# One score ahead of a turned tile on TensorE, and one more copy of a turned tile on VectorE in every fifth unit of an attention kernel

## The reference, cut to what matters

```python
q, k, v = proj(Wq), proj(Wk), proj(Wv)
scores = einsum('bhsd,bhtd->bhst', q, k) * scale
scores = where(mask, -inf, scores)
attn = softmax(scores, axis=-1)
out = einsum('bhst,bhtd->bhsd', attn, v) @ Wo.T
xn = out / rms(out) * rms_scale
x = x + xn * (1 + sc) + shift
x = x + rotate(x)
```

## Time and profile before

| | us |
|---|---|
| median of 3 runs | 815.74 (813.84 to 818.13) |
| the profiled execution | 813.31 |
| its span | 811.5 |
| TensorE busy | 796.2 (98%) |
| VectorE busy | 609.0 (75%) |
| ScalarE busy | 607.5 (75%) |
| GpSimd busy | 514.1 (63%) |

### The profile page before, as it was taken

One profiled execution on the slowest core, in us unless ns is written; L12 is line 12 of the kernel. 1 busy time (PEld: TensorE's weight loads), 2 busy tenths in 40 slices (PEclk: granted clock), 3 DMA queues, 4 the chain that ended last, 5 costly groups with the idle time before them and its releaser, 6 DMA issues.

```text
span 811.5 us, 16319 instructions
## 1 busy us (share of the span) xinstructions
PE 796.2 (98%) x4864; PEld 594.1 (73%) x4864; DVE 609.0 (75%) x1492; ACT 607.5 (75%) x1511; POOL 514.1 (63%) x371
## 2 busy tenths in 40 slices
PE   9999999999999899999999999999999999999987
PEld 6788888888887677677767776777677767776764
DVE  4612314213237799999999999999999999999866
ACT  6222323222326899999999999999999999999881
POOL 0899993000000011278888888888878888888894
PEclk9999999999999999999999999999999999999999
DMA  8964545546377988988999899999998999889301
GB/s 284 343 233 183 207 163 224 178 172 220 146 285 254 344 283 288 342 325 296 322 323 333 303 325 335 316 320 307 314 337 302 304 339 314 302 305 326 103 27 53
DMA packets 90575, 216.62 MB, mean 267 GB/s; under 512 B 10600, under 2 KB 11240, under 8 KB 82304
## 3 DMA queue, kind: packets, MB, share of 16 engines
q1 hardware_dynamic: 90352, 215.41, 75.8%
q10 hardware_dynamic: 144, 0.26, 0.1%
HBM read 133.81 MB, written 81.82 MB: 266 GB/s over the span
## 4 chain that ended last, share of the span: by engine, by line
PE 41%; ACT 36%; issue 9%; POOL 6%; DMA 3%; DVE 3%; SPq 1%; ACTq 0%; DVEq 0%; POOLq 0%
ACT probs L182 25%; PE banks L551 10%; PE banks L550 10%; PE banks L552 10%; ACT turned_probs L1129 7%; PE banks L889 3%; POOL late L769 3%; PE banks L924 3%; PE banks L163 3%; ACT o_T L1161 2%; DMA blocks_scratch<-staged_blocks 2%; POOL late L1267 1%; ACT inv_T L1145 1%; DMA turned_probs<-blocks_scratch 1%; PE banks L938 1%
## 5 line engine op out<-in xcount | busy, mean ns | idle before, releaser
L182 ACT ACTIVATE probs<-probs,least 128x512 f32<-128x512 f32 x512 | 393.8, 850 | 0.0
L174 DVE CUSTOM_DVE_ANT_0 probs<-banks,mask_bias 128x512 f32<-128x512 f32 x512 | 328.2, 682 | 14.5 <-PE banks L163 12.3
L889 PE MATMUL banks<-ident,probs 128*128 128x128 f32 x1568 | 230.2, 273 | 0.0
L889 PEld LDWEIGHTS banks<-ident,probs 128*128 128x128 f32 x1568 | 190.6, 140 | 42.1 <-issue 7.7
L163 PE MATMUL banks<-k_rows,q_rows 128*128 128x512 f32 x496 | 198.4, 452 | 0.2 <-issue 0.2
L1129 ACT ACTIVATE turned_probs<-banks 128x512 f32<-128x512 f32 x263 | 179.9, 712 | 8.5 <-PE banks L924 4.5
L182 ACT ACTIVATION_READ_ACCUMULATOR probs<-probs,least 128x1 f32 x512 | 168.0, 328 | 0.0
L477 DVE SCALAR_TENSOR_TENSOR late<-banks,late 128x512 fp32r<-128x512 f32 x64 | 43.9, 689 | 154.5 <-ACT late L414 154.5
L769 POOL TENSOR_TENSOR late<-rot,late 128x2048 f32<-128x2048 f32 x28 | 128.9, 4602 | 0.6 <-DVE late L1056 0.6
L414 ACT ACTIVATE late<-banks 128x512 fp32r<-128x512 f32 x64 | 38.2, 598 | 117.7 <-PE banks L552 110.6
L924 PE MATMUL banks<-turned_probs,v_sb 128*32 128x512 f32 (+1 forms) x1088 | 117.0, 570 | 6.2 <-DMA turned_probs<-blocks_scratch 4.6
(11 more groups left out here) (137 smaller groups left out, 1338.1 us busy)
## 6 DMA issues: line engine op xcount, KB each, us to landing
q_rows<-q_scratch SPq DMA_DIRECT2D x64, 512.0 KB, 6.5
k_rows<-k_scratch SPq DMA_DIRECT2D x62, 512.0 KB, 7.3
blocks_scratch<-staged_blocks SPq DMA_DIRECT2D x120, 256.0 KB, 4.6
turned_probs<-blocks_scratch SPq DMA_DIRECT2D x120, 256.0 KB, 3.5
q_scratch<-late SPq DMA_DIRECT2D x64, 256.0 KB, 2.3
k_scratch<-late SPq DMA_DIRECT2D x64, 256.0 KB, 2.3
out<-late SPq DMA_DIRECT2D x29, 256.0 KB, 4.9
raw<-in_xT SPq DMA_DIRECT2D x7, 1024.0 KB, 5.7
```

What stands on the lines that cost most here:

```text
L174: dve.tensor_tensor_reduce(self.probs[:, n % RING, :], self.ps[:, n % SCORE_BANKS, :], self.mask_bias[:, c, :], 1.0, 3e38, ALU.add, ALU.mi ...
L182: act.activation(self.probs[:, n % RING, :], self.probs[:, n % RING, :], ACT.Exp, bias=self.least[:, n % 32:n % 32 + 1], scale=-1.0, accum ...
L889: last = pe.transpose(turn_bank("tile", n)[:, j * P:(j + 1) * P], probs[:, n % RING, j * P:(j + 1) * P], ident[:, :])
```

## The change

In the early and whole units the three scores of place 7 become one at place 6 and two at place 7. In whole units whose number is a multiple of five (5, 10, 15, 20, 25) tile 0 is copied by VectorE.

```diff
-         "whole": (1, 2, 1, 0, 1, 0, 0, 3, 1, 1, 1, 0, 2, 0, 2, 1),
+         "whole": (1, 2, 1, 0, 1, 0, 1, 2, 1, 1, 1, 0, 2, 0, 2, 1),
-BY_ACT = "".join(BY_ACT[kind] for kind in KIND)
+MORE_BY_DVE = '0--0--1011011011'
+BY_ACT = "".join(MORE_BY_DVE if kind == "whole" and v % 5 == 0 else BY_ACT[kind] for v, kind in enumerate(KIND))
```

More of the change, by code:

```diff
@@ L61 @@
 SCORES = {"first": (0, 1, 4, 2, 2, 0, 1, 0, 2, 0, 0, 2, 0, 0, 1, 1),
-         "early": (1, 2, 1, 0, 1, 0, 0, 3, 1, 1, 1, 0, 2, 0, 2, 1),
-         "whole": (1, 2, 1, 0, 1, 0, 0, 3, 1, 1, 1, 0, 2, 0, 2, 1),
+         "early": (1, 2, 1, 0, 1, 0, 1, 2, 1, 1, 1, 0, 2, 0, 2, 1),
+         "whole": (1, 2, 1, 0, 1, 0, 1, 2, 1, 1, 1, 0, 2, 0, 2, 1),
          "half0": (1, 0, 2, 0, 1, 1, 1, 2),
```

## The result

| | before | after |
|---|---|---|
| median of 6 runs each, us | 815.59 (812.19 to 818.13) | 827.09 (825.72 to 828.07) |
| profiled execution | 813.31 | 828.07 |
| its span | 811.5 | 826.3 |

The ratio is 1.0154, with a 95% interval of 1.0133 to 1.0176: **the change makes the kernel slower**, by 11 to 14 us. The quotient of the two medians alone is 1.0141, inside that interval. The two profiled spans are 14.8 apart, the medians 11.5: the execution profiled before lies 2.3 under its median, the one after 1.0 above. The spans serve here to find the places, the ratio for the size.

What follows compares the result with a forecast made beforehand. ScalarE, with no idle time in whole units, was taken to set the pace. 5 x 2.1 = +10.5, -0.4 and +0.3 give +10.4, so 823.7 from 813.31; with the median's step of 2.4, 826.1 us, range 821 to 830.

Steps and rivals of the forecast that it cites:

- The copy stands and waits for the values of the unit before, 1.90: VectorE, unit 15: tile 0's copy, reached at 505.38, can't start before 507.28, a new wait of 1.90 us.
- What is queued behind it waits too: VectorE's queue is strictly in order, so its masks stand still behind the waiting copy.
- Tile 10's mask 2.50 late, its exponential 1.33: Unit 15: VectorE's mask 2.50 us late against 1.17 to spare, so ScalarE loses 1.33 at tile 10's exponential.
- +2.1 per unit and nothing given back later: Each of five units 2.1 us longer; later units, full on ScalarE, give none of it back.
- The signs: Profile after: about 9 us idle before VectorE's copies, about 2.6 on ScalarE in each of five units, which last 18.3.
- Part A: One score ahead of tile 6's turn: 0 in units full on ScalarE, -0.4 us over units 1 to 4.
- +0.3 for unit 5's late load: SyncE, unit 5: later block stores delay loads and the values needing them; +0.3 us taken, bounds 0 and 1.6.
- Behind the copy on VectorE stand three transposes, the rescale, and tile 10's mask: VectorE, unit 15: three transposes at 0.60 and the rescale at 0.63 follow the copy, putting the mask at 510.32.
- part B: Tile 0's copy from ScalarE (0.48 us) to VectorE (0.60) in five units; forecast loss 5 x 2.1 = +10.5.
- the three scores held up by masks for 1.93: TensorE, unit 15: the last of three scores waits for tile 11's mask until 512.29, 1.93 us late.
- The rival: TensorE's clock falls to its lower level for a unit: about 15 us more in each of five, 890; chance 0.01.
- the 0.9 and 1.2 that I had: TensorE would stand some 0.9 and 1.2 us in each of the five units.

Runs made afterwards that it cites:

- experiment 5: Changed kernel plus, in units 5, 10, 15, 20, 25, eight unread TensorE matmuls just ahead of its wait for the rescale; ratio 1.0121 to the unchanged kernel.
- Experiment 3: Changed kernel, but VectorE takes tile 0's copy later, behind the block transposes and the rescale; ratio 0.9997 to the unchanged kernel.
- experiment 4: Changed kernel, but in the five units the rescale stands at place 1, ahead of the waiting copy; ratio 1.0113 to the unchanged kernel.
- experiment 2: Changed kernel with the old order of scores, so only the five copies moved to VectorE; ratio 1.0163 to the unchanged kernel.

## Why the prediction was right, and where it was not

**Right: the sign, the place, and the sum but for the clock.** 826.1 was forecast, 827.09 measured, inside 821 to 830. Measured against its own ratio the rise is 12.5 (10.8 to 14.4) for a forecast 10.4, just below the interval. The forecast's 10.4 is the sum of a kernel whose clock stays up, and experiment 5 is in effect that kernel: 9.9 (8.2 to 11.5). That the median still came within 1 us of the forecast is in part luck, as a loss that was put at nothing came on top.

- *The copy stands and waits for the values of the unit before, 1.90.* Measured 1.84 in unit 15. Experiment 3 shows that the wait, not the 0.60 of work, is what costs.
- *What is queued behind it waits too.* The rows of VectorE show three transposes, rescale and mask in one piece behind the copy; none overtakes it. So the trace agrees with the in-order rule of the Trainium skill (PSUM — Partial Sum Buffer, section "Engine vs sequencer instructions") for VectorE too.
- *Tile 10's mask 2.50 late, its exponential 1.33.* Measured 2.35 and 1.14 in unit 15, 1.26 for the exponential in unit 20.
- *+2.1 per unit and nothing given back later.* At full clock 1.83 and 2.05 in the changed kernel, 1.99 to 2.05 in experiment 5. Later units stay at 16.16 to 16.28.
- *The signs: 9 us of idle before VectorE's copies, 2.6 us of idle on ScalarE in each of the five, units of 18.3.* Measured 10.9, five times; at full clock, in unit 20, 18.30 - 16.34 = 1.96 on ScalarE and a length of 18.25, but in three of the five 19.74 to 19.86.
- *Part A nothing in full units, -0.4 in units 1 to 4.* Measured 0.12 in each of units 2 to 4, 0.36.
- *+0.3 for unit 5's late load.* Not seen: in unit 5 the length grew by 1.83, less than in the others, and the next unit's values didn't wait for a DMA. The lower bound, 0, was right.

**The step that failed for the path: "Behind the copy on VectorE stand three transposes, the rescale, and tile 10's mask."** The rescale was counted as 0.63 of delay for the mask and not asked who waits for it: the add on GpSimd was looked at, TensorE's projection, which needs the rescale's bank, was not. It stands 1.87 us in each unit and holds up the turn of tile 6 behind it, whose copy the walk through part B passes over: in unit 20 that copy is 1.90 late, so tile 12's exponential, which follows it, no longer waits for its mask, and only 0.16 is added up to the copy of tile 8. At full clock the sum comes out alike by either path (1.7 to 1.9 in experiment 4 without it, 2.0 in experiment 5 with it), so the 2.1 was right partly by luck: I had the three scores held up by masks for 1.93, where the projection ahead of them already held TensorE for 1.87, and the two cover each other.

**The term that was mis-sized: the clock.** The rival was there, with a chance of 0.01 and a price of 15 us a unit, and both were wrong. I took unit 5's 1.36 us of standing at 1.00 as evidence for all standing, though the standing that the change adds is longer, and in one piece: 1.87, and not the 0.9 and 1.2 that I had. The clock fell in three of five units, for some 3.3 us of slow work each, and that costs 3.6 - 2.0 = 1.6 each, 4.8 in the execution profiled: a third of the loss. A single stand without a fall proves little. The trace of the kernel before has a longer one, in unit 1, at full clock as well, and the trace of the second kernel with tile 11's copy (`v % 3`) has one with a fall behind it in unit 5, which that edit leaves alone. TensorE's timeline and the window behind it, before:

```profile
276.04 3.21 PE L924 MATMUL banks<-turned_probs,v_sb 128*32 128x512 f32 x28 [2.37 <-DMA turned_probs<-blocks_scratch]
```

```profile
276.50:281.00 4.50, 4.50 (x42) 2.23 (x35) 2.18 (x6) 2.09 (x7) 0.00 (x0) 1.00 0.89 293
```

and with tile 11's copy in every third unit:

```profile
343.88 2.43 PE L925 MATMUL banks<-turned_probs,v_sb 128*32 128x512 f32 x12 [2.84 <-DMA turned_probs<-blocks_scratch]
```

```profile
344.30:347.70 3.40, 3.40 (x20) 1.08 (x16) 1.07 (x2) 0.87 (x4) 1.27 (x1) 0.50 0.95 387
```

So a stand of 2.37 us had no fall behind it where six of ten of 1.87 had one, in the changed kernel and in experiment 2 together: the length of a stand does not settle it. The forecast should have spread the chance: something like one unit in two.

Dose and response, from the traces of unit 15, at full clock: tile 10's mask 0.23 late costs nothing (experiment 3), 2.12 late costs 1.69 (4), about 2.4 late costs 2.03 (5). The forecast's 1.17 of lead would leave 0.95 and 1.2 for tile 10's exponential, and it is 0.89 and 1.23 late. The rest of the cost comes from the waits behind it, which have to be counted: in experiment 4 those that the prediction names (tile 12's exponential, tile 8's copy), in experiment 5, where the projection still waits for the rescale, tile 6's copy.

What stays open: why the clock fell in units 10, 15, 25 of one kernel and 5, 15, 25 of the other behind the same 1.9 us, and not behind 2.37 us in the kernel before. No run here tells it.

## What to carry to other kernels

When an instruction moves from one in-order engine to another, look first at what it waits for and when the new engine gets there: 0.60 us of work cost nothing four instructions later and 2 to 3.6 us where it was put. Then walk the whole queue behind the wait and ask of each instruction who waits for it, on every engine, as a bank that is not emptied stops TensorE as surely as a missing input. And a saving on the engine that is full in the profile is only worth what the next loop leaves: here three engines are within 0.2 us of each other per unit, and the 0.48 taken from ScalarE at tile 11 came back in the next unit, most of it at its head as a wait for TensorE.

## What the runs showed of the hardware that was not expected

A stand of TensorE of 1.87 us in one piece was followed by work at the lower level (granted clock 0.50 from 517.4 to 520.7 us) in three of five units, and in unit 20 by work at full clock. In the kernel before stands of 1.36 and 2.37 us were followed by full clock, and in one of the other kernels a stand of 2.84 us by the lower level (0.50 from 344.3 to 347.7 us). At the lower level four 128-column transposes span 1.05 us instead of 0.60, and two 512-column scores 1.20 instead of 0.71. Matmuls whose result nobody reads kept the clock at 1.00 in all five places.
